# Query scores of the second query block: one matmul over both key blocks, and the causal mask accumulated last

## What is computed

```python
Q, K, V = (jnp.einsum('bsd,hkd->bhsk', x, W) for W in (WQ, WK, WV))
scores = jnp.einsum('bhqd,bhkd->bhqk', Q, K) / math.sqrt(d_k)
scores = jnp.where(causal, scores, -jnp.inf)
probs = jax.nn.softmax(scores, axis=-1)
attn = jnp.einsum('bhqk,bhkv->bhqv', probs, V)
...
x = x + _layernorm(_L0_attn_ref(_layernorm(x, axis=-1), WQ, WK, WV, WO), axis=-1)
x = x + _layernorm(_L0_ffn_ref(_layernorm(x, axis=-1), centroids, ln_g, ln_b, w1, b1, w2, b2), axis=-1)
```

## Time and profile before

| what | us |
|---|---|
| median of 3 runs | 561.53 |
| the three runs | 557.7, 561.53, 565.01 |
| span of the profiled execution | 559.6 |
| PE busy in it | 391.9 |
| VectorE busy in it | 369.9 |

### The profile page before, as it was taken

How to read it: one execution, slowest core, us unless ns; L and a number is a source line. 1 busy time by engine, 2 the same in 40 slices (tenths; PEclk the granted TensorE clock), 3 DMA queues, 4 the chain that set the end, 5 groups by cost and what they waited for, 6 DMA issues and landing times.

```text
span 559.6 us, 13677 instructions
## 1 busy us (share of the span) xinstructions
PE 391.9 (70%) x3737; PEld 307.1 (55%) x3738; DVE 369.9 (66%) x1422; ACT 251.1 (45%) x548; POOL 250.3 (45%) x349
## 2 busy tenths in 40 slices
PE   3287769679679797797796796874196768776630
PEld 2155547557457576575575574653185557665530
DVE  7568558578586586687786775876465666666650
ACT  2125445446445454454554553641074555554520
POOL 5612444343445544535545444565214444444453
PEclk9999789899798798898998887995589997899985
DMA  6635454254252352342451442121321111111100
GB/s 181 119 50 86 110 95 83 74 96 73 38 97 61 59 86 72 54 86 62 67 86 50 74 82 69 57 101 39 126 68 56 59 50 56 46 56 53 57 18 5
DMA packets 33398, 39.96 MB, mean 71 GB/s; under 512 B 7561, under 2 KB 27149, under 8 KB 31808
## 3 DMA queue, kind: packets, MB, share of 16 engines
q1 hardware_dynamic: 28400, 32.02, 28.4%
q0 software_dynamic: 2832, 6.53, 3.4%
q10 hardware_dynamic: 2112, 0.80, 0.8%
HBM read 25.18 MB, written 14.61 MB: 71 GB/s over the span
## 4 chain that ended last, share of the span: by engine, by line
PE 35%; DMA 24%; POOL 13%; issue 11%; DVE 9%; ACT 2%; DVEq 1%; POOLq 1%; ACTq 1%; SPq 1%
DMA shift_rows<-nmT 17%; POOL out_x L521 7%; PE ST L819 5%; PE O L840 4%; DMA aug<-shift_rows 4%; POOL rsz L529 4%; PE S L806 3%; PE M L852 3%; PE S L799 2%; PE S L796 2%; PE M L867 2%; PE ST L828 2%; PE O L844 2%; PE S L801 2%; DMA aug<-qk_parts 2%
## 5 line engine op out<-in xcount | busy, mean ns | idle before, releaser
L1060 DVE TENSOR_REDUCE nmf<-S 128x2 f32<-128x512 f32 (+1 forms) x192 | 130.8, 683 | 91.6 <-PE S L799 58.0
L592 ACT ACTIVATE p<-ST 128x1024 f32<-128x1024 f32 x64 | 65.7, 1027 | 58.3 <-PE ST L819 57.6
L819 PE MATMUL ST<-aug 128*128 128x256 bf16 x256 | 43.6, 299 | 57.5 <-DMA aug<-shift_rows 57.5
L429 POOL TENSOR_SCALAR_AFFINE_SELECT p<-p 128x512 f32<-128x512 f32 x64 | 41.0, 640 | 91.5 <-ACT p L592 91.3
L521 POOL DMA_INDIRECT out_x<-vaug,ids x39 | 40.3, 1034 | 72.8 <-DVE vez L1403 68.8
L819 PEld LDWEIGHTS ST<-aug 128*128 128x128 bf16 x256 | 24.4, 104 | 63.3 <-issue 35.4
L806 PE MATMUL S<-aug 126*128 126x128 bf16 x512 | 53.9, 231 | 0.0
L433 POOL TENSOR_SCALAR_AFFINE_SELECT p<-p 128x512 f32<-128x512 f32 x64 | 41.6, 649 | 19.9 <-ACT p L596 17.1
L990 PE MATMUL O<-w_tab,vaug 128*128 x312 | 45.6, 292 | 0.8 <-ACT vaug L729 0.8
L806 PEld LDWEIGHTS S<-aug 126*128 126x128 bf16 x512 | 43.2, 105 | 4.4
L840 PE MATMUL O<-p,vaug 128*32 128x256 f32 x512 | 44.1, 414 | 0.9 <-POOL p L429 0.9
(11 more groups left out here) (149 smaller groups left out, 950.8 us busy)
## 6 DMA issues: line engine op xcount, KB each, us to landing
qk_parts<-qkp SPq DMA_DIRECT2D x16, 384.0 KB, 2.8
aug<-qk_parts SPq DMA_DIRECT2D x32, 192.0 KB
x_all<-xs_rows SPq DMA_DIRECT2D x39, 131.0 KB, 2.1
aug<-qk_parts SPq DMA_DIRECT2D x32, 128.0 KB
aug<-qk_parts SPq DMA_DIRECT2D x32, 64.0 KB
w_tab<-in_w1t SPq DMA_DIRECT2D x8, 256.0 KB, 2.6
w_tab<-in_w2t SPq DMA_DIRECT2D x8, 256.0 KB, 3.1
out_x<-vaug,ids POOLq DMA_INDIRECT x39, 2.3
```

The costliest lines, as they stand in the source:

```text
L429: g.affine_select(out=v, in_=v, compare_op=ALU.is_ge, fill=0.0, base=0, pattern=[[0, 4], [1, P]], channel_multiplier=-1).then_inc(s["sel0" ...
L592: a.activation(p0[:, gr % 2], ST0[:, :, :], ACT.Exp, scale=SCALE).then_inc(s["exp0"], 1)
L819: last = mm(ST0[:, j], kaug[:, p, h, 0:P], qaug[:, p, h], start=True, stop=True)
L1060: v.tensor_reduce(dst, S[:, n % 2].rearrange("p (j n) -> p j n", j=k), op=ALU.max, axis=AX_X, negate=True).then_inc(s["red"], 1)
```

## The change

In the turns u = 1 and u = 2, the four score matmuls of 128 columns (two heads, two key blocks each) become two of 256 columns, one for each head, with all 256 keys as moving operand. The first of them opens the bank. The mask matmul, with the same operands and the same output columns as before, moves from the front of the turn to its end, adds to the scores, and carries the signal to VectorE. Turn u = 0 stays as it is.

```diff
@@ -798,13 +798,11 @@
                         h = 4 * gr + j
                         last = mm(bank[:, j * P:(j + 1) * P], q[:, h, 0:P], k[:, h, 0:P], start=False, stop=(j == 3))
                 else:
-                    mm(bank.rearrange("p (j c n) -> p j c n", j=2, c=2)[:, :, 1], identb[:, :], causal[:, 0:2],
-                       start=True, stop=False)
                     for j in range(2):
                         h = 4 * gr + 2 * (u - 1) + j
-                        for kb in (0, 1):
-                            last = mm(bank[:, j * SEQ + kb * P:j * SEQ + (kb + 1) * P], q[:, h, P:SEQ],
-                                      k[:, h, kb * P:(kb + 1) * P], start=False, stop=(j == 1 and kb == 1))
+                        mm(bank[:, j * SEQ:(j + 1) * SEQ], q[:, h, P:SEQ], k[:, h, :], start=(j == 0), stop=False)
+                    last = mm(bank.rearrange("p (j c n) -> p j c n", j=2, c=2)[:, :, 1], identb[:, :], causal[:, 0:2],
+                              start=False, stop=True)
                 last.then_inc(s["s_r"], 1)
```

## The result

| | before | after |
|---|---|---|
| median of 20 runs, us | 562.43 | 561.27 |
| lowest and highest, us | 557.7, 567.86 | 558.26, 564.2 |
| span of the profiled execution, us | 559.6 | 557.8 |

The median fell by 1.2 us, 0.2%. The comparison of the two kernels, however, gave a ratio of after to before of 1.0095, with a 95% interval of 1.0062 to 1.0129: by that number the change costs 0.95%. The ratio counts only runs within 1.5% of the fastest of the same kernel, the medians all of them. The two readings contradict each other, and the experiments begin with that.

The account below looks back on a forecast made before the run. PE, the busiest engine, was taken to alternate with the DMA of shift_rows. Saving 0.3 to 0.4 us in the loop and at most 0.06 before it, -0.4 in sum, gave 559.2 us; 1.9 above that, 561.1 us, range 556 to 566.

Parts of the forecast that it names:

- Within 2%: Whole kernel: time within about 11 us of the kernel before, chance 0.93; faster 0.03, slower 0.04.
- hidden altogether: Rival: the saving, 0.03 us of PE per pass, vanishes in the varying write of shift_rows; 561.5 us, chance 0.24.
- the saving of a turn: Groups u = 1 and 2 at full clock: 0.334 us becomes 0.327, saving 0.007 us, between 0 and 0.015.
- The columns that stream through PE stay the same: Each group u = 1 or 2 streams 768 columns through PE before and after, despite fewer matmuls and loads.
- the rival of the loads: Weight loads of 0.098 us space the score matmuls; 0.10 us saved per path group, about 555 us, chance 0.04.
- The strided addition: Mask matmul at the group's end, adding with a gap between column runs: 0.109 us chosen, upper bound 0.21 us.
- The strided addition stalls: Rival: the mask matmul at each group's end costs 0.10 us more on 60 path groups; 567 us, chance 0.05.
- The map of the path: Per pass, three or four early groups before L781 count at full clock, 45 to 60 in 15 passes; others nothing.
- the clock could fall otherwise: Rival: low-clock stretches in the passes change, 0.85 us per pass; 555 us (chance 0.04) or 567 us (0.05).
- three groups are worth nothing: Head group 2's u = 2 and both of 3, behind L781 before PE's idle time: time saved there gains nothing.
- The signs named: Expected: PE's nmf waits near 1 us, L819's wait some 57 us; failure if low-clock stretches or the shift_rows write change.

Follow-up runs that it names:

- the filled pair: Changed kernel and kernel before, each with 14 unused matmuls of 512 columns in PE's idle time at the end of each pass: 544.07 and 544.63 us.
- split64: Changed kernel with each score matmul of 256 columns cut into four of 64: 564.22 us, ratio 1.0065.
- mask_last: Kernel before with only the mask matmul moved to the end of the turn, four score matmuls of 128 columns kept: 561.98 us, ratio 1.0001.
- early4: Changed kernel with the mask matmul issued four times in four early turns of each pass: 564.33 us, ratio 1.0044.
- late4: Changed kernel with the mask matmul issued four times in the three turns behind the transpose of the row maxima: 556.98 us, ratio 0.9895.
- mask_twice: Changed kernel with the mask matmul issued twice at the end of each turn u = 1 and 2: 564.97 us, ratio 1.0049.
- no_mask: Changed kernel without the mask matmul in turns u = 1 and 2: 557.22 us, ratio 0.9942.
- fill14: Changed kernel with 14 unused matmuls of 512 columns at the end of each pass, in PE's idle time: 544.07 us, ratio 0.9684.
- fill8: Changed kernel with 8 unused matmuls at the end of each pass, in PE's idle time: 550.51 us, ratio 0.9806.

## Why the prediction was right or wrong

- **The time.** 561.1 was forecast, 561.27 is the median of the first 20 runs, 562.86 and 558.91 those of the repeats. "Within 2%", at 0.93, holds. That the first median lies 0.2 us off is luck, with single runs 10 us apart, and the time cannot tell the forecast from "hidden altogether" (561.5 us).
- **The sign.** A gain of 0.4 us was forecast. The ratio of the first comparison, 1.0095, has the changed kernel slower, beyond its interval; its medians and means, two repeats and the filled pair do not. What the starts show of a gain is 0.1 us, which no comparison here can see: the runs confirm neither direction.
- **The failed term: the saving of a turn.** "The saving is 0.334 - 0.327 = 0.007 us for a group" took L819's distance of 0.109 us for all three matmuls. They measured 114, 108 and 112 ns, 334 together: saving 0 in front of the scores by key, and 3 ns in front of the values. On the path's turns that is 0.1 us in place of 0.4. The step did say that it lies between 0 and 0.015 us; taking the middle made a sign out of a rounding.
- **The columns.** "The columns that stream through PE stay the same" is what decided. It held against the rival of the loads, which split64 decides: eight loads for two cost some 0.015 us. The rule of the Trainium skill (TensorE: Matmul & The Clock Gate, Back-to-back issue gap), 81 ns for a pair of load and 128 columns, is not borne out here: such pairs start 55 ns apart.
- **The strided addition.** Chosen at 0.109 us; measured 112 ns, and mask_last 1.0001. "The strided addition stalls" had up to 0.10 us more per turn, of which 3 to 5 ns are there. The rule of the Trainium skill that non-contiguous patterns slow matmuls (PSUM — Partial Sum Buffer, Specifications) does not show with runs of 128 columns: 112 ns for 256 columns with the gap, 108 without.
- **The map of the path.** Early turns count, late turns don't: early4 and late4 at equal clock differ by 1.26 us for 1.31 us. That part was right.
- **The clock.** The rival said that the clock could fall otherwise, at 0.85 us per pass, and that nothing in the change pushes it. For the change that held (0.89 and 0.90 in the loop). But "three groups are worth nothing" was wrong in general: PE work behind L781 shortens the idle time, and 1 us of it per pass made the kernel 5.9 us faster (4.6 by the means of all runs). The expectations for mask_twice, early4 and no_mask came out two to eight times too large. They were made with a fixed clock; in early4 the clock accounts for some 10 of the 17 us that are missing, by an estimate (half of 56.0 - 36.9 us). In no_mask it is not the clock, which was at 0.88 in the loop for 0.89: in the traced execution the work got shorter as forecast and the DMA part longer. For mask_twice it stays open. The prediction read the low clock as a circumstance of a pass, when it was the largest item that an edit in these runs moved.
- **The signs named.** PE's waits for nmf, which were to stay near 1 us, are 2.1 us in the kernel after, but 1.3 and 1.2 us in its repeats. The stretches of lower clock and the DMA part differ between executions of one kernel (125.0 to 131.0 us for the latter), so neither can serve as the sign of failure that the prediction made of them.
- **What a measurement can tell.** The 2% was cautious for the medians, but the ratios with their intervals gave 0.9986 and 1.0074 for identical programs, where the means of all runs give 0.9993 and 1.0006.

## What to carry to other kernels

Cutting the same columns into fewer or more matmuls did next to nothing for PE here, as the loads hide behind them: look at the distance between starts, and count columns. Where PE waits several us in each pass and the granted clock is 0.5 behind the wait, the lever is the wait: filling it with matmuls that nobody needs gave 3.2% here, some forty times the edit's forecast. And before a difference below 1% is explained, time the unchanged kernel against itself in more than one session, and ask which runs a ratio counts: one fast run moved it by 0.5%.

## What the runs showed of the hardware that I had not expected

- Pairs of load and matmul with 64 bf16 columns follow each other after 0.03 us at full clock, though a load lasts 0.096 to 0.099 us in the turn shown of split64: the loads overlap in their records.
- The granted clock of the loop went with PE's waits for the shift rows: 0.88 with 66.5 us in all (no_mask), 0.89 with 57.5 us, 0.93 with 49.4 us (late4), 0.96 with 34.5 us (fill8) and 0.99 with 19.0 us (fill14).
- Behind a turn the values, which use another tile of the array (128*32 for 128*128 in the timeline), start 149 ns after a matmul of 128 columns and 203 ns after one of 256, where the scores by key start after 55 and 112 ns.
- VectorE's one-element-wide `eneg` step, 0.16 us elsewhere, took 1.81 us once in the trace of the kernel after and held PE for 0.37 and 1.09 us in that pass. Such a hiccup is larger than the whole forecast; its cause is open.

```profile
235.78 1.81 DVE L1163 TENSOR_SCALAR eneg<-eneg  x1
...
238.62 0.39 PE L803 MATMUL S<-aug 126*128 126x256 bf16 x2 [0.37 <-DVE nmf L1058]
...
241.00 0.66 PE L850 MATMUL M<-ident,oT 128*128 128x128 f32 x4 [1.09 <-DVE on L1085]
```
